# Layer-norm rows of the self-attention and feed-forward stages: transposed on VectorE and by transfers within SBUF

## The reference

```
x = x + cross_attention(layernorm(x), ctx, ctx, mask)    # 16 heads of 32, 512 keys per sequence
x = x + self_attention(layernorm(x))                     # 16 heads of 32, 64 keys, biases on Q, K, V, O
x = x + feed_forward(layernorm(x))                       # relu(x W1^T + b1) W2^T + b2, W1 and W2 rounded to -1, 0, 1
```

## Time and profile before

| | |
|---|---|
| time, median of 3 runs | 1744.25 us (1743.09 to 1746.99) |
| span of the profiled execution | 1745.7 us; no time of its own is listed for it |
| mean granted TensorE clock | 0.993 |
| cross-attention, about | 0 to 772 us |
| self-attention, about | 772 to 1264 us |
| feed-forward, about | 1264 to 1746 us |

### The profile page before, as it was taken

The page is one execution under the profiler, slowest core; times in us unless marked ns, Lnnn a source line. Parts: engine busy times, 40 slices in busy tenths (PEclk is TensorE's granted clock), DMA queues, the critical chain, the costliest instruction groups (busy, mean ns, idle before and its releaser), DMA issues.

```text
span 1745.7 us, 38877 instructions
## 1 busy us (share of the span) xinstructions
PE 1689.3 (97%) x16268; PEld 1416.7 (81%) x16268; DVE 1032.7 (59%) x1492; ACT 701.8 (40%) x1689; POOL 216.0 (12%) x300
## 2 busy tenths in 40 slices
PE   6899999999999999998999999999899999999999
PEld 4688878788878788787888898989688888888887
DVE  3655556555565555667677777776674445544543
ACT  2555555665555566566422222323222222222221
POOL 1000000000000000122111121211032012202200
PEclk9999999999999999999999999999999999999999
DMA  6011111111111111333010101001101101100000
GB/s 218 13 62 62 62 62 61 52 59 62 61 62 55 48 54 54 132 132 139 26 49 24 48 24 41 31 27 57 51 31 49 49 1 49 48 17 31 25 24 24
DMA packets 48668, 95.00 MB, mean 54 GB/s; under 512 B 5792, under 2 KB 14112, under 8 KB 47264
## 3 DMA queue, kind: packets, MB, share of 16 engines
q1 hardware_dynamic: 48544, 93.16, 15.7%
HBM read 67.97 MB, written 25.17 MB: 53 GB/s over the span
## 4 chain that ended last, share of the span: by engine, by line
PE 90%; DVE 6%; issue 2%; ACT 2%; DMA 0%; DVEq 0%; SPq 0%; ACTq 0%
PE project L339 49%; PE project L1273 13%; PE scores L685 4%; PE scores L1791 3%; PE probs_t_psum L1791 3%; PE scores L1789 3%; PE probs_t_psum L1789 3%; PE probs_t_psum L694 3%; PE attended_t L711 2%; PE probs_t_psum L1379 2%; PE scores L491 1%; PE attended_t L1398 1%; DVE ff_weight_scratch L1224 1%; PE attended_t L1252 1%; DVE w_ternary L1227 1%
## 5 line engine op out<-in xcount | busy, mean ns | idle before, releaser
L1273 PE MATMUL project<-ff_xt,w_ternary 128*128 128x512 f32 x1024 | 256.4, 393 | 0.0
L1273 PEld LDWEIGHTS project<-ff_xt,w_ternary 128*128 128x128 f32 x1024 | 190.0, 188 | 38.4
L1282 ACT ACTIVATE hidden<-project,b_sb 128x512 f32<-128x512 f32 x128 | 88.2, 689 | 326.1 <-PE project L1273 326.1
L887 ACT ACTIVATE cross_scores_probs<-cross_scores_probs,exp_bias,logit_scale 128x128 f32<-128x128 f32 x256 | 122.6, 482 | 97.9 <-DVE exp_bias L1033 97.9
L339 PE MATMUL project<-self_xt_hi,self_w_hi 128*128 128x256 f32 x512 | 148.4, 290 | 3.2 <-DVE self_xt_lo L502 2.3
L339 PE MATMUL project<-self_xt_lo,self_w_hi 128*128 128x256 f32 x512 | 145.1, 283 | 0.0
L339 PE MATMUL project<-self_xt_hi,self_w_lo 128*128 128x256 f32 x512 | 145.0, 283 | 0.0
L887 ACT ACTIVATE cross_probs<-cross_scores,exp_bias,logit_scale 128x128 f32<-128x128 f32 x256 | 122.8, 483 | 0.4 <-DVE exp_bias L1033 0.4
L339 PE MATMUL project<-ctx_hi,cross_w_hi 128*128 128x512 f32 x256 | 107.0, 418 | 15.2 <-DVE ctx_lo L1052 15.2
L339 PE MATMUL project<-cross_w_hi,ctx_hi 128*128 128x512 f32 x256 | 108.8, 425 | 0.0
L339 PEld LDWEIGHTS project<-self_xt_hi,self_w_hi 128*128 128x128 f32 x512 | 98.4, 192 | 6.3 <-DVE self_xt_lo L502 2.6
(11 more groups left out here) (175 smaller groups left out, 4098.5 us busy)
## 6 DMA issues: line engine op xcount, KB each, us to landing
ctx_raw<-in_ctx SPq DMA_DIRECT2D x64, 256.0 KB, 4.0
cross_xt_raw<-in_x_t SPq DMA_DIRECT2D x64, 128.0 KB, 2.2
cross_x<-in_x SPq DMA_DIRECT2D x32, 256.0 KB, 3.0
x<-cross_x SPq DMA_DIRECT2D x32, 256.0 KB, 2.0
self_x<-x SPq DMA_DIRECT2D x32, 256.0 KB, 2.8
ff_w_raw<-in_w SPq DMA_DIRECT2D x2, 4096.0 KB, 13.8
x<-self_residual SPq DMA_DIRECT2D x32, 256.0 KB, 2.0
ff_x<-x SPq DMA_DIRECT2D x32, 256.0 KB, 3.4
```

Of the source, the lines that this page charges most:

```text
L887: last = nc.scalar.activation(c_p[buf][:, cols], c_s[buf][:, cols], ACT.Exp, bias=exp_bias[:, buf, g:g + 1], scale=logit_scale[:, parity(u ...
L1273: last = nc.tensor.matmul(PJ[m % 2][:], w1_q[:, c, cols], x_t[parity(v)][:, c, :], start=(c == 0 and x_t is fxt_hi), stop=(c == DC - 1 and ...
L1282: nc.scalar.activation(h_raw[:, m % 2, :], PJ[m % 2][:], ACT.Relu, bias=b1_sb[:, m:m + 1]).then_inc(h_relu, 1)
```

## The change

Normalised rows stay in SBUF. Per pair of tiles VectorE runs one instruction that transposes each 32x32 block of the 128x1024 tile (`ln_blocks`), and SP issues four transfers from 32 partitions each back into the tile of normalised rows (`ln_gather`), so that partition 4k + j holds features c*128 + j*32 + k. The rows of Wq, Wk, Wv and W1 are put in the same order on the host (`interleaved`). ScalarE rounds and VectorE subtracts the whole pair at once, 128x1024 from SBUF. TensorE's transposes X0 and X1, those of the feed-forward and of the borders are removed, with their PSUM banks. In the feed-forward the matmuls read their 512 columns in runs of 32. New waits: the transpose on the normalised rows and on the gather before; the gather on the transpose; the rounding on the gather and, in the self-attention, on V1; Q0 and the first hidden block on the remainder. In the last two steps of the cross- and self-attention the layer-norm work is placed anew on VectorE, ScalarE and SP. Some tiles lie elsewhere in SBUF, and a scratch area for transfers is set to 1024.

```
+        def ln_blocks(xn, blocks):
+            return nc.vector.transpose(
+                blocks.rearrange("p (j i r) -> p i j r", j=4, r=32),
+                xn.rearrange("p t (c j k) -> p (t c) j k", j=4, k=32))
+        def ln_gather(e, xn, blocks, done):
+            whole = xn.rearrange("p t (a n) -> p t a n", a=4)
+            for a in range(4):
+                e.dma_start(whole[:, :, a, :], blocks[32 * a:32 * a + 32, :]).then_inc(done, 16)
...
+        def self_x_hi(e, v):
+            wait(e, G.ln_in, total(v, 64, 64))
+            nc.scalar.activation(sxt_hi[:], sx_chunks, ACT.Copy).then_inc(G.xt_hi, 1)
+        def self_x_lo(e, v):
+            wait(e, G.xt_hi, total(v, 1, 1))
+            nc.vector.tensor_tensor(sxt_lo[:], sx_chunks, sxt_hi[:].bitcast(F32), ALU.subtract) \
+                .then_inc(G.xt_lo, 1)
...
 cross_sync, last step
+                        self_ln_gather(e, S_SECOND)
                         load_self_x(e, Unit(1, 0))
...
 cross_dve, last step but one
                 values_out(u, v, 0)
+                if not ahead:
+                    self_statistics(S_FIRST)
                 maxima(u, 3)
                 values_out(u, v, 1)
+                if not ahead:
+                    self_ln_normalise(e, S_FIRST)
+                    self_ln_transpose(e, S_FIRST)
                 divide(u, 2)
...
 self_sync
+                if kind == "full":
+                    self_ln_gather(e, later(u, 2))
...
+                    ff_ln_gather(e, F_FIRST, 1)
                 store(u, 0, kind)
+                if kind == "last_but_one":
+                    ff_ln_gather(e, F_FIRST, 0)
...
 self_pe, step
                     v_proj(u, 1, kind, lambda: attend_waits(u, 1))
-                    x_transpose(u, later(u, 2), 0)
                     attend(u, 1)
...
                     o_proj(u, 0, kind)
-                    x_transpose(u, later(u, 2), 1)
...
 self_act
+            def x_hi(u, v):
+                full(u, "V1")
+                self_x_hi(e, v)
...
 self_dve, last step
                 maxima(u, 0)
+                ff_x_lo(e, F_FIRST, 0)
                 values_out(None, u, 0)
                 divide(u, 0)
+                for t in range(2, FT):
+                    ff_ln_normalise(e, F_FIRST, t)
+                ff_ln_transpose(e, F_FIRST, 1)
                 residual(later(u, -1), 1, "last_but_one")
                 maxima(u, 1)
...
 self_dve, step
                     self_ln_normalise(e, w)
+                    self_ln_transpose(e, w)
                 maxima(u, 1)
...
-                    x_lo(u, w, 0)
+                    self_x_lo(e, w)
...
                 residual(u, 0, kind)
                 a_lo(u, 1)
-                if kind == "full":
-                    x_lo(u, w, 1)
...
 ff_pe, step
                     contract(u, m)
-                    if more and m in (3, 5, 7, 9):
-                        x_transpose(v, (m - 3) // 2)
...
 ff_dve, step
-                        if m in (2, 4, 6, 8):
-                            ff_ln_normalise(e, v, (m - 2) // 2)
-                        if m in (3, 5, 7, 9):
-                            t = (m - 3) // 2
-                            ff_x_lo(e, v, t, XB[t % 2])
+                        if m in (2, 3, 6, 7):
+                            ff_ln_normalise(e, v, (0, 1, 2, 3)[(2, 3, 6, 7).index(m)])
+                        if m in (3, 7):
+                            ff_ln_transpose(e, v, m // 4)
+                        if m in (5, 10):
+                            ff_x_lo(e, v, m // 5 - 1)
```

More of the change, by code:

```diff
@@ L463, in build, with self_ln_transpose, self_ln_gather @@
         SLOT = [(pair % 2) * 4 + pair // 2 for pair in range(PAIRS)]
[L465 to L469 removed]
+        sx_chunks = sxn[:].rearrange("p t (a c r) -> p c (t a) r", a=4, r=32)
+        tokens_of = lambda xt, c, first, n: (xt[:, c].rearrange("p a r -> p (a r)")
+                                             [:, first:first + n])
+        def self_ln_transpose(e, v):
+            wait(e, G.xn, total(v, NT, NT))
+            wait(e, G.ln_in, total(v, 64))
+            ln_blocks(sxn[:], s_ln_t[:]).then_inc(G.ln_t, 1)
+        def self_ln_gather(e, v):
+            wait(e, G.ln_t, total(v, 1, 1))
+            ln_gather(e, sxn[:], s_ln_t, G.ln_in)
         def self_qk_products(e, bank, n, w, before_last=None):
@@ L736, in self_qk @@
                 if n == 0 and w == 1:
-                    for t in range(NT):
-                        b, before = K.banks.at(u, f"x{t}", "last")
-                        e.wait_ge(C.pj_free[b], before + 1)
+                    e.wait_ge(G.xt_lo, 1)
                 self_qk_products(e, bank, n, w).then_inc(C.pj_full[bank], 1)
@@ L815, in step @@
                     scores(u, 1)
-                    for t in range(NT):
-                        self_xt(u, t)
                     self_qk(u, 0, 1)
@@ L939, in step @@
                 queries_out(u, 1)
+                if not ahead:
+                    self_x_hi(e, S_FIRST)
                 a_hi(u, K.nt - 1)
             def last_step(u):
-                for t in range(NT):
-                    bank = full(u, f"x{t}", "last")
-                    self_x_hi(bank, t).then_inc(G.xt_hi, 1)
                 exponentials(u, 0)
@@ L1107, in last_step @@
             def last_step(u):
-                self_ln_normalise(e, S_FIRST)
                 maxima(u, 0)
                 residual(later(u, -1), K.nt - 1, "last_but_one")
-                for t in range(NT):
-                    bank = full(u, f"x{t}", "last")
-                    self_x_lo_out(bank, t, t + 1, C.pj_free[bank])
                 maxima(u, 1)
@@ L1431, in last_step @@
                 v_proj(u, 1, "last")
+                transposes(u, 0)
+                attend_waits(u, 0)
+                attend(u, 0)
+                o_proj(u, 0, "last")
+                transposes(u, 1)
+                e.wait_ge(fxt_lo_ready, 2)
                 for name in ("V0", "V1"):
@@ L1590, in full @@
                 return bank
-            def x_lo(u, v, t):
-                bank = full(u, f"X{t}")
-                wait(e, G.xt_hi, total(v, NT, t + 1))
-                self_x_lo(bank, t).then_inc(G.pj_free[bank], 1)
             def a_hi(u):
@@ L1750, in step @@
                             .then_inc(fx_in[parity(w)], 16)
+                if kind != "last":
+                    for n in range(2):
+                        ff_ln_gather(e, later(u, 1), n)
                 for t in range(FT):
```

245 lines of the change are left out of this document (101 added, 144 removed).

## The result

The changed kernel takes 1793.95 us, the median of four runs (1792.09 to 1797.44); the kernel before took 1745.18 us beside it (1743.09 to 1746.99). The ratio is 1.0285, with a 95% interval of 1.0271 to 1.0298: some 49 us slower, where +4.8 was forecast. The sign was right, the time lies far outside the range.

The account below looks back on a forecast made before the run. TensorE was taken to set the pace, VectorE three quarters full. Terms -13.2 + 6.6 + 0 + 3.15 + 1.2 + 7.0 = +4.8 us gave 1750.5 on the span, 1749 on the median; own range 1745 to 1755, wide 1735 to 1762.

Parts of the forecast that it names:

- The sign: Whole kernel: slower was the likeliest direction, chance 0.52, against 0.28 for same and 0.20 for faster.
- Feed-forward, -13.2: Feed-forward: 28 removed TensorE transpose groups save 0.47 us each, 13.2 us; the rest there is covered.
- rival (4): Feed-forward: TensorE reads runs of 32 slower, 0.01 us more in 1024 products, 10 us: 1759; chance 0.08.
- The loop, +6.6: Self-attention loop: the whole-pair split delays quantising and the second output projection by 0.55 us in twelve units, +6.6 us.
- VectorE's transpose, 1.22: Ahead of a unit's second softmax half: 128x1024 transpose takes 1.22 us, bounds 0.69 and 2.4; cover about 1.5.
- rival (3): VectorE's transpose takes 2.4 us, breaking the cover in 14 units, +13, borders +4: 1766; chance 0.10.
- The gather, 4 us: Four transfers on SP: about 4 us from transpose's end to landed data, bounds 3 and 6; free in the loop.
- Cross to self, +3.15 and +1.2: Cross-to-self border: first query projection 3.15 us later behind store and gather, including the first border; clock fall adds 1.2.
- the forecast of 4.35: Start to the loop's first trip: predicted lengthening of 4.35 us, from the border terms +3.15 and +1.2.
- Self to feed-forward, +7.0: Self-to-feed-forward border: VectorE's added work delays V1 6.9 us, clock falls, O0 moves to 1259.9: +7.0 us.
- rival (2): Borders: the clock holds, so they cost 3.15 + 2.0, sum -1.4: no change, 1743; chance 0.25.
- Rival (1), O1 released by O0: Loop: O0's end releases O1, about 0.8 us earlier; -10 in 12 units instead of +6.6: 1732; chance 0.17.

Follow-up runs that it names:

- run 9: Kernel before with only the change's feed-forward part, units 1 to 7, split rows written by tokens so TensorE reads one run of 512: 1730.97 us, ratio 0.9924.
- run 8: Changed kernel with loop code moved by 144 instructions, feed-forward operand in one run, and VectorE's gathered-row subtraction behind self_at_lo: 1743.45 us, ratio 0.9984.
- run 1: Changed kernel with its loop's code moved by 144 TensorE instructions in a branch never taken: 1766.41 us.
- run 7: Changed kernel with loop code moved by 144 instructions and VectorE's subtraction of the gathered rows moved behind self_at_lo: 1757.10 us.
- run 3: Changed kernel with split feed-forward rows written by tokens, so TensorE reads its 512 columns in one run: 1777.46 us.

## Why the prediction was wrong

In order of its steps.

*Feed-forward, -13.2: the term was right, the rival beside it was weighed wrong.* Run 9 gives -14.7 with no other part of the change, run 8's stage from O0 to the end (1263.71 to 1742.3) is 14.2 shorter than before. What took it back in the changed kernel is rival (4), to which I gave 0.08 with "nothing in the rows shows such a read". Its price of 0.01 us a product was nearly exact: 1.90 less 1.81 over eight products is 0.011, 12 us in all. That was luck, since no row stood under the 0.01; and the rival left out that the contractions would slow down as well, which adds 3. An operand read in a way that no row shows should have had bounds and a share in the sum, as the VectorE transpose had, and not a small chance at the end.

*The loop, +6.6: the mechanism was right, and something outside the sum came on top.* The waits stand where they were put. In run 1, V1's last matmul ends at 935.65 and the quantising starts at 938.00, 2.35 us later where 2.33 was forecast:

```profile
935.26 0.39 PE L347 MATMUL project<-self_w_hi,self_xt_lo 128*128 128x512 f32 x1
...
938.00 0.48 DVE L1232 TENSOR_SCALAR ff_weight_scratch<-ff_w_raw,thresholds 128x512 f32 x1
```

O1, at 942.15, comes 6.50 us behind that end of V1 instead of 5.93, +0.57 where +0.55 was forecast. It waits 1.67 us for `self_at_lo` (forecast about 1.85), since a part of the 1.07 us for the transposes comes back where they stood (2.95 us from the start of O0 to what follows it, instead of 2.86). A unit is 30.67 us, +0.75: the other 0.18 stands between O1 and the next V1, where the forecast had no change, and is not explained.

The failed step is that this +6.6 was the whole term of the loop. The prediction took the removed transposes as nothing but time saved, and put what their removal does to the place of the loop's code at nothing, without a reason. Its last word on instructions, that the moved tiles, the reordered rows and the smaller scratch "cost no instruction", looks only for instructions added; the change took 107 away, and the loop's place follows from all that stand ahead of it. What the runs showed in its place is 27.5 us by the medians (run 1). Between the profiles of run 1 and of the changed kernel, the latter the slowest of its four executions, the loop's stage differs by 400.46 - 369.18 = 31 us. Of these 1.6 are the first trip, which ran at a granted clock of 0.66 (848 to 853 us) in the changed kernel and at 1.00 in run 1. The rest is five reloads of 5.9 us each: 1.4 to 2.0 at the return, 2.0 to 2.9 behind the 25th score product and about 2 in the projection at the lower clock level, less the wait for `self_at_lo` that they hide. No term of the forecast held that; its range of 27 us was made from the mechanisms I had listed.

*VectorE's transpose, 1.22.* Confirmed, 1.246 (groups: shapes, count | busy, mean ns | idle before):

```profile
L427 DVE STREAM_TRANSPOSE self_blocks_t<-self_x_norm 128x1024 f32<-128x1024 f32 x16 | 19.9, 1246 | 1.7
```

Taking the nearest row with the same number of elements was the right choice between 0.69 and 2.4, and rival (3) falls: in the loop no group of transposed probabilities waits. The Trainium skill's figure (VectorE: DVE Perf Modes, The three transpose paths) would have made 2.5 us by my estimate; this instruction took half of that.

*The gather, 4 us.* Longer. Four issues take 2.63 us on SP (the row at 770.09 below), 0.66 each instead of 0.44, and a landing 2.9 us instead of 2.2:

```profile
self_x_norm<-self_blocks_t SPq DMA_DIRECT2D x64, 128.0 KB, 2.9
```

At the last border it came to 5.9 us from the transpose's end to ScalarE (below), next to the upper bound of 6. In the loop it costs nothing, as forecast: the four issues of a unit start at 924.77 in run 1 and ScalarE takes the rows at 935.77, when V1 lets it.

*Cross to self, +3.15 and +1.2.* Q0 was put at 778.65, behind the gather, and that behind the store (order of time, SP's issues and TensorE; first the changed kernel, then run 1):

```profile
769.70 0.34 SPq L647 DMA_DIRECT2D x<-cross_x  x1
770.09 2.63 SPq L435 DMA_DIRECT2D self_x_norm<-self_blocks_t  x4
...
778.33 0.55 PE L347 MATMUL project<-self_xt_hi,self_w_hi 128*128 128x256 f32 x1 [6.01 <-DVE self_xt_lo L531]
```

```profile
772.12 0.34 SPq L647 DMA_DIRECT2D x<-cross_x  x1
...
780.60 0.55 PE L347 MATMUL project<-self_xt_hi,self_w_hi 128*128 128x256 f32 x1 [5.86 <-DVE self_xt_lo L531]
```

The order is the one that was written down, and TensorE idles about 6 us instead of 3.85. That Q0 stands at 778.33 is luck. The store of the earlier trace rows, at 771.56, was forecast 0.6 later, and Q0 then 6.5 us behind it (3.94 before). In the changed kernel the store is 1.9 us earlier, which no step had, and Q0 follows it after 8.63 us; in run 1 the store is 0.6 later, as forecast, and Q0 follows after 8.48, 2 us later than forecast. The 2 us are the gather: from its first issue to ScalarE's rounding it takes 5.8 us in the changed kernel and 5.6 in run 1, where 3.6 were summed. The stretch from 778 to 782 us has a granted clock of 0.50. Up to the first trip of the loop the forecast of 4.35 compares with 2.1 in the changed kernel, 2.9 in run 1, 1.4 in run 7 and 5.2 in run 8. These profiles also differ in when the clock fell, and no run takes the stage apart.

*Self to feed-forward, +7.0.* Run 1: from the last O1 to O0 51.77 us instead of 45.32, +6.45. Its V1 comes 40.27 us behind that O1 instead of 32.70, +7.6 (forecast +6.9), and from V1 to O0 it takes 11.50 instead of the 12.7 forecast. In the changed kernel the chain reads as it was written down:

```profile
1274.45 1.25 DVE L427 STREAM_TRANSPOSE ff_blocks_t<-ff_x_norm 128x1024 f32<-128x1024 f32 x1
...
1275.73 3.63 SPq L435 DMA_DIRECT2D ff_x_norm<-ff_blocks_t  x4
...
1281.57 1.06 ACT L1269 ACTIVATE ff_xt<-ff_x_norm 128x1024 fp32r<-128x1024 f32 x1 [2.41 <-DMA ff_x_norm<-ff_blocks_t]
...
1289.28 0.65 DVE L1631 TENSOR_TENSOR self_residual<-project,self_residual 128x512 f32<-128x512 f32 x1
```

V1 follows at 1289.98, and the clock falls as said, so rival (2) is out:

```profile
1290.00:1295.00 5.00, 5.00 (x12) 3.95 (x13) 2.29 (x2) 0.00 (x0) 0.00 (x0) 0.50 0.68 197
```

*Rival (1), O1 released by O0,* was what run 7 brought about: there O1 waits 0.41 us, and a unit is 0.27 us shorter than before, where the rival had 0.8. It took a move of one line in VectorE's order, which the change did not have.

*The chances.* A slip: (1) and a fifth of (2) add up to 0.22 for faster, not 0.20.

So of the 49 us, some 27 are the place of the code (run 1) and 14 to 16.5 the short runs (run 8 against run 7, and run 3). The rest, 5 to 8, is near the 4.8 that the forecast had summed: 1793.95 - 27.5 - 16.5 = 1750 against 1749. This adds up two runs; no run has both edits and not run 7's. And the sum is better than its parts: with the loop's code moved, the stages are +2.9, +7.7 and +6.5 (run 1) where 4.35, 6.6 and 7.0 were forecast, and the feed-forward without the short runs is -14.2 (run 8) instead of -13.2. The borders were not undone one at a time.

## What to carry to other kernels

When instructions are added or removed ahead of a long loop, compare the instruction queue's packets and look for "issue" waits at the loop's start, before explaining anything by data; move the loop's code with instructions in a branch that is never taken, and see whether the time follows. Where a new layout is to save work, pay for it on the engine that has room: the short runs that cost TensorE 12 to 15 us cost ScalarE and VectorE nothing. Try the parts of a change apart: one of these two was worth 14.7 us, the other lost 12.5 even when mended. And look at the borders, where stages hand over, apart from the loop: they lost nearly all of that 12.5 in run 8, while its loop took no longer than that of run 9.

## What the runs showed of the hardware that I had not expected

A loop of TensorE that lay over seven blocks of 256 instructions ran its trips without being loaded again; 8 instructions into an eighth, none or two of five returns were loaded anew; 56, 104 and 140 in, all five, with nine packets of 16.4 KB each time. A reload cost 5 to 6 us: a wait of 1.0 to 2.9 us at the return, one of 0.8 to 3.3 at the first block's edge, and behind them, in most trips, a few microseconds at the 1.2 GHz level.

A moving operand of 512 float32 columns in 16 runs of 32 cost TensorE 0.011 us more a matmul, in 2 runs of 256 nothing; and the matmuls that follow, with contiguous operands of their own, were slower too (0.395 instead of 0.389 us for the first kind). Why these were slowed is not settled.

VectorE transposed 128x1024 float32 in 32x32 blocks in 1.246 us; a subtraction of 128x1024 took 1.222 in the same trace.
